# Cross-attention probabilities packed 80 columns a head into ten full tiles, V as a block matrix built by transfers, and a new order of steps on all engines

## What is computed

```
x = x + attn(_layernorm(x))            # part A
Q = (queries @ W_q.T).reshape(b, sq, 16, 16).transpose(0, 2, 1, 3)
K, V = the same of ctx_1024 (77 tokens) with W_k, W_v
scores = einsum('bhqd,bhkd->bhqk', Q, K) / 4
scores = where(mask, scores, -1e10)
attention = softmax(scores, axis=-1)
heads_out = einsum('bhqk,bhkd->bhqd', attention, V)
x = x + (heads_out as [b, sq, 256]) @ W_proj.T + b_proj
x = x + ffn(_layernorm(x))             # part F
```

## Time and profile before

| | us |
|---|---|
| median of three runs | 1768.66 (1768.13 to 1780.2) |
| profiled execution | 1782.64 |
| its span | 1780.9 |
| TensorE matmuls busy | 1669.9 (94% of the span) |
| VectorE busy | 1284.1 (72%) |
| ScalarE busy | 1027.2 (58%) |
| GpSimd busy | 828.4 (47%) |

### The profile page before, as it was taken

The page is one execution under the profiler, slowest core; times in us unless marked ns, Lnnn a source line. Parts: engine busy times, 40 slices in busy tenths (PEclk is TensorE's granted clock), DMA queues, the critical chain, the costliest instruction groups (busy, mean ns, idle before and its releaser), DMA issues.

```text
span 1780.9 us, 34265 instructions
## 1 busy us (share of the span) xinstructions
PE 1669.9 (94%) x12064; PEld 1509.9 (85%) x12064; DVE 1284.1 (72%) x3060; ACT 1027.2 (58%) x2671; POOL 828.4 (47%) x937
## 2 busy tenths in 40 slices
PE   3699999999999999999999999999999999999986
PEld 3588898988888988888898888888888888898875
DVE  4566767777777777777777777677777777777642
ACT  2355555566566566665656666565666666666541
POOL 3354543454544454454445545444554544455320
PEclk9799999999999999999999999999999999999988
DMA  4000000000000000000000000000000000000000
GB/s 115 3 7 9 15 15 15 1 15 15 15 16 15 12 4 15 15 15 15 15 15 2 15 15 15 15 15 15 2 15 15 15 15 15 15 1 16 9 7 12
DMA packets 44696, 26.61 MB, mean 15 GB/s; under 512 B 24432, under 2 KB 44528, under 8 KB 44528
## 3 DMA queue, kind: packets, MB, share of 16 engines
q1 hardware_dynamic: 44528, 24.43, 5.0%
HBM read 16.03 MB, written 8.39 MB: 14 GB/s over the span
## 4 chain that ended last, share of the span: by engine, by line
PE 70%; DVE 17%; issue 6%; ACT 5%; DMA 1%; POOL 1%; SPq 0%; ACTq 0%; POOLq 0%; DVEq 0%
PE bank L373 58%; DVE a_conv L800 8%; PE bank L379 5%; PE bank L607 4%; DVE x_nmax L925 2%; ACT x_xn L1097 2%; PE bank L684 2%; ACT x_prob L1244 1%; DVE f_wt L1002 1%; DVE f_th L1014 1%; DVE a_ssum L847 1%; DVE f_wt L1001 1%; DMA x<-in_x 1%; ACT x_K_stack L1212 1%; PE bank L461 1%
## 5 line engine op out<-in xcount | busy, mean ns | idle before, releaser
L1244 ACT ACTIVATE x_prob<-bank,x_nmax 128x77 f32<-128x77 f32 x1024 | 248.1, 328 | 170.0 <-DVE x_nmax L925 170.0
L373 PEld LDWEIGHTS bank<-x_Vx,x_probT 77*128 77x128 f32 x2048 | 256.7, 194 | 1.6
L373 PE MATMUL bank<-x_Vx,x_probT 77*128 77x17 f32 x2048 | 249.4, 255 | 0.0
L925 DVE TENSOR_REDUCE x_nmax<-bank 128x4 f32<-128x308 f32 x256 | 121.6, 475 | 176.9 <-PE bank L373 174.2
L800 DVE SCALAR_TENSOR_TENSOR a_conv<-a_raw,cw,a_conv 128x256 f32<-128x256 f32 x384 | 198.3, 589 | 11.4 <-POOL a_conv L1364 11.4
L1255 ACT ACTIVATE x_probT<-bank 77x512 f32<-77x512 f32 x256 | 152.4, 595 | 41.4 <-PE bank L607 41.0
L607 PE MATMUL bank<-ident,x_prob 128*77 128x128 f32 x1024 | 160.6, 280 | 5.5 <-ACT x_probT L1255 5.5
L1402 POOL TENSOR_TENSOR a_orinv<-a_ove,mhalf 128x8 f32<-128x8 f32 x32 | 53.3, 1665 | 211.7 <-DVE a_ove L865 211.7
L607 PEld LDWEIGHTS bank<-ident,x_prob 128*77 128x77 f32 x1024 | 122.3, 150 | 16.9 <-issue 11.1
L1339 POOL TENSOR_TENSOR x_rstd<-x_ve,mhalf 128x2 f32<-128x2 f32 x32 | 22.8, 711 | 217.3 <-DVE x_neg L755 217.3
L373 PE MATMUL bank<-x_K_bd,x_Q_stack 128*128 128x308 f32 x256 | 96.6, 378 | 20.5 <-ACT x_prob L1244 19.7
(11 more groups left out here) (254 smaller groups left out, 5512.3 us busy)
## 6 DMA issues: line engine op xcount, KB each, us to landing
x<-in_x SPq DMA_DIRECT2D x32, 256.0 KB, 2.9
out<-x SPq DMA_DIRECT2D x32, 256.0 KB, 2.1
ctxT<-in_ctxT SPq DMA_DIRECT2D x32, 77.0 KB, 2.5
keep<-in_mask SPq DMA_DIRECT2D x32, 19.2 KB, 2.5
f_s<-in_fWu SPq DMA_DIRECT2D x2, 256.0 KB, 5.6
a_AT<-in_Wv SPq DMA_DIRECT2D x1, 256.0 KB, 3.0
a_okn<-in_Ws SPq DMA_DIRECT2D x1, 256.0 KB, 3.7
a_qn<-in_Wg SPq DMA_DIRECT2D x1, 256.0 KB, 3.5
```

Of the source, the lines that this page charges most:

```text
L373: return pe.matmul(out, lhsT, rhs, start=start, stop=stop, skip_group_check=True)
L925: dve.tensor_reduce(nmax[:, u % 2, :], X0[:, 0:UH * S2].rearrange("p (h s) -> p h s", h=UH), AX.X, ALU.min).then_inc(on.x_max, 1)
L1244: ins = act.activation(prob[:, u % 2, i, :], X0[:, i * S2:(i + 1) * S2], ACT.Exp, scale=-1.0, bias=nmax[:, u % 2, i:i + 1])
```

## The change

Part X only, apart from the order:

- A head's 77 probabilities now lie at a pitch of 80 columns, so that 16 heads are 1280 columns, ten tiles of 128. A chunk's ten tiles are transposed in four groups (2, 3, 2 and 3 tiles) in place of sixteen tiles of 77: 20 transposes a row, not 32, each of 128 columns. ScalarE copies 128x256 or 128x384 in place of 77x512, still eight times a row.
- The product with V takes a tile at a time, with 128 partitions, against `x_Vbd`, a block matrix in which the 2 or 3 heads that share a tile have 17 columns each: 34 or 51 columns. The sums of a head that lies in two tiles add up in the bank. 20 products a row, not 32.
- `x_v` copies V into `x_Vtok`, and SyncE then issues 12 transfers a row from there into `x_Vbd` (77, 48, 29, 77, 16, 61, 64, 13, 77, 32, 45 and 77 partitions, two runs of 16 numbers each). The first `x_av` of a row waits for all twelve. There are two `x_Vbd`; their ones are loaded once with the weights (two transfers of 128x510).
- SyncE now loads x ahead of the store, and the context one body earlier.
- The mask's step `x_neg` stands apart from `x_kbd` on GpSimd and runs one body earlier. The transposed logits have a tile of their own. The tables of order on all engines are new.
- Row numbers are plain integers in place of a pair of half and parity; this changes no instruction.

```diff
+PITCH = 80
+NT = NH * PITCH // P
+GROUPS = (range(0, 2), range(2, 5), range(5, 7), range(7, 10))
+VW = 3 * (HD + 1)
...
-        Vx = sb("x_Vx", [S2, NH, HD + 1])
+        Vtok = sb("x_Vtok", [S2, NH, HD])
+        Vbd = [sb(f"x_Vbd_{i}", [P, NT, VW]) for i in range(2)]
...
-        prob = sb("x_prob", [P, 2, UH, S2])
-        probT = sb("x_probT", [S2, 2, UH, P])
+        prob = sb("x_prob", [P, NH * PITCH])
+        probT = sb("x_probT", [P, NT, P])
...
+            def x_vbd(r):
+                sp.wait_ge(on.x_v, upto(r))
+                if r > 1:
+                    sp.wait_ge(on.x_av_ps, upto(r - 2, NU))
+                dst, src = Vbd[r % 2], Vtok[:].rearrange("s (g h) e -> s g h e", g=2)
+                for s, n, h, t, p, col in V_PIECES:
+                    sp.dma_start(dst[p:p + n, t::NT // 2, col:col + HD], src[s:s + n, :, h, :]).then_inc(vbd_in, 16)
...
+                L(a_load); F(f_store); L(x_load); A(x_vbd)
...
-                for i in range(UH):
-                    ins = pe.transpose(X1[0:S2, i * P:(i + 1) * P], prob[:, u % 2, i, :], ident[:])
+                for i, t in enumerate(GROUPS[u % QU]):
+                    ins = pe.transpose(X1[:, i * P:(i + 1) * P], prob[:, t * P:(t + 1) * P], ident[:])
...
             def x_av(r, u):
                 c, q = divmod(u, QU)
                 if u == 0:
                     pe.wait_ge(on.x_v, upto(r))
+                    pe.wait_ge(vbd_in, upto(r, V_DMAS))
...
-                for i in range(UH):
-                    h = q * UH + i
-                    ins = mm(X2[:, h * (HD + 1):(h + 1) * (HD + 1)], probT[:, u % 2, i, :], Vx[:, h, :])
+                for t in GROUPS[q]:
+                    h, w = first_head(t) * (HD + 1), tile_heads(t) * (HD + 1)
+                    ins = mm(X2[:, h:h + w], probT[:, t, :], Vbd[r % 2][:, t, 0:w], start=(t == 0),
+                             stop=(t == NT - 1))
...
-                F(x_ot); A(a_vtok); A(a_qbd); X(x_k); X(x_xn); A(a_ktok); X(x_xnt); N(a_xn); F(f_xn); N(a_xnt)
+                A(a_et); F(x_ot); A(a_vtok); X(x_xn); A(a_ktok); X(x_k); X(x_xnt); N(a_xn); F(f_xn); X(x_v)
```

More of the change, by code:

```diff
@@ L226, in build @@
                      *[{s: sem(f"{s}_{n}") for s in "axf"} for n in NORM_STEPS.split()])
[L228 to L262, removed]
-            body(Row(last - 1, 1), Row(last - 1, 0), Row(last - 2, 1), Row(last - 2, 0))
-            body(None, Row(last - 1, 1), Row(last - 1, 0), Row(last - 2, 1))
-            body(None, None, Row(last - 1, 1), Row(last - 1, 0))
-            body(None, None, None, Row(last - 1, 1))
+        def upto(r, n=1, k=None):
+            return n * r + (n if k is None else k)
@@ new lines, in loaded, with first_head, tile_heads, pieces @@
+        def loaded(r, n=1):
+            return 16 * n * (r // 2 + 1)
+        def first_head(t):
+            return t * P // PITCH
+        def tile_heads(t):
+            return (t * P + P - 1) // PITCH + 1 - first_head(t)
+        def pieces():
+            found = []
+            for h in range(NH // 2):
+                s = 0
+                while s < S2:
+                    t, p = divmod(h * PITCH + s, P)
+                    n = min(S2 - s, P - p)
+                    found.append((s, n, h, t, p, (h - first_head(t)) * (HD + 1)))
+                    s += n
+            return found
@@ L268, in build, with row, iterations @@
+        V_PIECES = pieces()
+        V_DMAS = 16 * len(V_PIECES)
+        def row(i):
+            return i if 0 <= i < B else None
+        def iterations(body, others):
+            for i in range(B + 3):
+                body(row(i), row(i - 1), row(i - 2), row(i - 3))
+                if i == 0:
+                    others()
         block = ctx.enter_context(nc.Block())
@@ L366, in _ @@
+            for i in range(-1, B + 3):
+                body(row(i + 1), row(i), row(i - 1), row(i - 2), row(i - 3))
+                if i < 0:
+                    for dst, src in weights:
+                        sp.dma_start(dst, src).then_inc(ld_w, 16)
+                    for dst, src in other_weights:
+                        sp.dma_start(dst, src).then_inc(ld_v, 16)
             for i in range(2):
@@ L1125, in a_raw_qk @@
             def a_raw_qk(r):
-                if later(r):
-                    act.wait_ge(on.a_conv, upto(before(r), 3 * 4))
+                if r > 0:
+                    act.wait_ge(on.a_conv, upto(r - 1, 3 * 4))
                 act.wait_ge(on.a_qk_ps, upto(r))
@@ L1205, in x_k @@
             def x_k(r):
-                if later(r):
-                    act.wait_ge(on.x_kbd, upto(before(r)))
+                if r > 0:
+                    act.wait_ge(on.x_kbd, upto(r - 1))
                 act.wait_ge(on.x_k_ps, upto(r))
@@ L1267, in f_lgt @@
                 act.wait_ge(on.f_gate_ps, upto(r))
[L1268 to L1270 removed]
+                if r > 0:
+                    act.wait_ge(on.f_lg_ps, upto(r - 1))
+                act.activation(lgT[:], F1[0:NE, 0:T], ACT.Copy).then_inc(on.f_lgT, 1)
             def f_gap(r):
```

405 lines of the change are left out of this document (204 added, 201 removed).

## The result

| | kernel before | changed kernel |
|---|---|---|
| median, us | 1774.0 (1768.13 to 1780.2, 4 runs) | 1599.83 (1594.45 to 1601.51, 4 runs) |
| profiled execution, its span, us | 1782.64, 1780.9 | 1600.0, 1598.2 |
| mean granted clock | 0.965 | 0.986 |

The ratio is 0.9013, with a 95% interval of 0.8966 to 0.9059.

A forecast was written before the change was run, and what follows sets the result against it. TensorE was taken as the bound: 30 bodies each 3.4 us shorter (102), plus 4 at the end, minus 1 at the start, save 105 us; 1782.6 becomes 1677.6, scaled to 1664 us, range 1636 to 1718.

The forecast's parts named there:

- 46.5 us of work a body: TensorE's work a body after fewer products with V and fewer transposes: 50.1 us less 3.55.
- R2: TensorE's transposes: loads cost by their columns, 0.166 us per wide transpose; saving 2.2 us a body, 1700 us; chance 0.11.
- a wait of about 1.0 us stands in place of the 0.61: TensorE in the softmax: the moved convolution makes it wait about 1.0 us before unit 6's scores.
- 0.6 us at part A's output: TensorE's wait before the transpose of part A's output, behind a_conv, a_gate and GpSimd: 0.6 us a body.
- chain of 9.0 us: From unit 4's scores to unit 6's: reductions, convolution, a_qkv, exponentials and handovers take 9.0 us against TensorE's 8.0.
- 2 us for each of the two bodies: End of the kernel: each of two last bodies with part X but not part N saves 2 us.
- 0.47 us each, twelve 6 us: SyncE's queue: V's transfers keep it 0.47 us each, start 0.5 apart, twelve taking 6 us.
- sum of 8.9: V's transfers: 6 us issue plus 2.9 landing, 8.9 us from x_v's copy, hidden before the first product with V.
- R3: TensorE's first product with V waits for late transfers; 42 us more in all, 1811 us; chance 0.04.
- idle time before `x_xn`: TensorE's 0.54 us wait before transposing part X's normalised input goes, by x_xn before x_k's copies and an earlier x load.
- R1: Softmax: reduction and exponentials still hold TensorE, so half the saving goes; 1.7 us a body, 1716 us; chance 0.17.
- R4: Whole body: everything is hidden, waits fall to 0.4 us, a body of 46.9 us, 1628 us; chance 0.10.

The follow-up runs named there:

- before_elo_out: Kernel before, with ScalarE's high-half copy and GpSimd's Elo subtraction moved later, the subtraction out of VectorE's convolution: 1745.0 us, ratio 0.9855.
- elo_in_conv: Changed kernel with ScalarE's copy of E's high half ahead of the gate, so GpSimd's subtraction runs beside VectorE's convolution: 1614.4 us, one execution.
- pack_fill: pack_old_xv plus 18 unused identity multiplications a body where TensorE idles: 1701.47 us, ratio 0.9569.
- before_fill: Kernel before plus 14 unused identity multiplications a body, 8 ahead of unit 4's scores and 6 ahead of V: 1767.15 us, ratio 0.9934.
- xv_late: Changed kernel with ScalarE's copy of V moved back behind the exponential of a_okn: 1728.8 us, one execution.
- pack_old: Changed kernel with the earlier order on TensorE, VectorE, ScalarE and GpSimd, V's copy at its old late place: 1887.0 us, one execution.
- xk_first: Changed kernel with ScalarE's four copies of K put ahead of x_xn: 1644.5 us, one execution.
- load_late: Changed kernel with SyncE's store put ahead of the load of x again: 1680.8 us, one execution.
- pack_old_xv: Changed kernel with the earlier order on TensorE, VectorE, ScalarE and GpSimd, but V's copy early on ScalarE: 1810.88 us, ratio 1.0144.

## Why the prediction was wrong in size

*TensorE's work.* "46.5 us of work a body": 46.4 measured. The ten wide passes at 0.104 us and the transposes at 0.11 are the terms as priced. Rival R2, loads that cost by their columns, is out: 77 columns had a mean of 280 ns, 128 have 278, and three transposes, 0.5 us by R2's price, take 0.33. By the Trainium skill's rule ("TensorE: Matmul & The Clock Gate", section "LDWEIGHTS (loading the stationary operand)") a load takes its number of columns divided by 1.2 ns, by my estimate 107 ns for 128 columns and 64 ns for 77. The 0.11 us a transpose agree with the first. The second does not show in the traces: the transposes with 77 columns took 0.09 to 0.11 us as well.

*The waits.* This is the first step that failed: "a wait of about 1.0 us stands in place of the 0.61", and 0.6 us at part A's output, 1.6 in all; 0.16 is listed, about 0.3 in all. The chain of 9.0 us carried the convolution over at 6.20 us, a duration that belonged to the old neighbourhood. before_elo_out and elo_in_conv show that GpSimd's subtraction was in it for 1.02 us, and the clip for 0.35. With 4.83 the chain is 7.6 us against 8.0 of TensorE's work, and no wait is due; with 5.50, in elo_in_conv, 0.3 were due and 0.26 came. The 0.6 us at part A's output were a guess at a size: 0.16 came. Per body the forecast missed 4.81 - 3.4 = 1.4 us, in these 28 bodies 134.7 against 28 x 3.4 = 95.2, so 39.5 us.

*The clock.* The second one: the sum has no term for it, although stand at 0.99 and 0.81 and the mean of the profiled execution was 0.965. The kernel before lost about 27 us in its bodies to it and the changed one loses none; with the changed kernel's short first body (44.85 us) that is the 28.6 us. Its cause is shown only in kind: pack_fill shows that extra work in idle time can keep the clock up, before_fill took back 12 us of the 27, and before_elo_out almost none. Why the changed kernel loses none stays open.

*Start and end.* Outside these 28 bodies the forecast had two more full ones, "2 us for each of the two bodies" of the end, and minus 1: 9.8 us, where 19.5 were saved. The end gave 8.9 and the start 10.6. The granted clock rose there too, from 0.84 to 0.93 up to the first of these loads and from 0.90 to 0.92 behind the last; how the gain divides between the order and the clock was not tried.

Together 39.5 + 28.6 + 9.7 = 78 us, the difference between 182.7 and 105.

*V's transfers.* "0.47 us each, twelve 6 us": they take 0.82 each and 9.85 us in all, two thirds more. (The two starts in the earlier trace rows are 0.43 us apart, not 0.5.) The landing, put at 2.9 us, was 1.2, read from xv_late. The sum of 8.9 became 11.1, and the margin covered it: data at about 752.6, first product at 758.90. Rival R3 needed a later copy, and in pack_old it was there.

*The idle time before `x_xn`.* Gone as said; xk_first brings 1.6 us of it back by ScalarE's order alone, and load_late 2.1 us by SyncE's.

*The rivals.* R1 happened at its price of 1.7 us a body in pack_old_xv, about half of it by the softmax: it was right in size for the packing under the old order and wrong for the new one. R4 had the body (46.9) and missed the time by the clock and the start.

## What to carry to other kernels

A duration read from a trace belongs to what ran beside it: before it is carried to a new place, look at which instruction of a group is long and what the other engines did then. Work taken from the bounding engine is worth only a part of itself until the order lets the others keep up (1.7 of 3.5 us here), and can be worth less than nothing where the clock falls with the new gaps (pack_old_xv). Give the granted clock a term of its own: count the bodies that are longer than the usual one. Where gaps can't be closed, multiplications that nobody reads are a cheap test of what the clock costs, and sometimes a gain.
